# Set-up, linear attention and experts of a two-layer transformer merged into one part with four written orders

## The chip, the cores and the metric

The kernel runs on one core of a Trainium2 chip. The metric is the device time of one execution in microseconds (us), median over runs. The engines are TensorE (PE in the profile, its weight loads PEld), VectorE (DVE), ScalarE (ACT), GpSimd (POOL) and SyncE (SP), which here only issues DMAs. Each has its own queue and works it off strictly in the order in which the program wrote it; semaphores hold them together.

## The reference, cut to what matters

`x` is (4, 1024, 128), fp32. Two layers of attention and feed-forward follow each other, each with adaptive layernorm. What the change touches is layer 0:

```python
mod = (silu(L0_c) @ L0_wmod).reshape(4, 6, 1, -1)     # sa, ca, ga, sb, cb, gb; the same for layer 1
ga = (2 * (ga >= 0) - 1) * maximum(abs(ga), 0.25)      # gb too
h = layernorm(x) * (1 + ca) + sa
q = softmax(split_heads(h @ Wq + bq), axis=-1) * s     # 16 heads of 8
k = softmax(q, axis=-2) * s
ctx = einsum('bhnd,bhne->bhde', k, split_heads(h @ Wv + bv))
x = x + ga * (merge(einsum('bhnd,bhde->bhne', q, ctx)) @ Wo + bo)
h = layernorm(x) * (1 + cb) + sb
comb = ...   # sigmoid scores, best 2 of 4 groups, best 4 of 16 experts
x = x + gb * (sum over experts of comb * (silu(h @ w1.T) * (h @ w3.T)) @ w2.T, and one shared expert)
```

Layer 1 (a windowed attention and two blocks of a local transformer) stays as it is.

## The kernel before

`X` holds all 32 tiles of 128 tokens in SBUF. A batch has eight tiles. Each part is a block of its own, and all engines meet at its end.

`setup` (from L192) loads constants and `X`, multiplies the conditioning by `wmod` and spreads the rows of it that are needed over 128 partitions (`rowB`), then clamps the first gate `ga` there as a 128x512 tile on VectorE. `modT` holds the same values as columns.

`linear_attention` (from L272) loops twice over a pair of batches, `bi`; the two batches of a pair are two streams. A pair is worked in two turns `g` of four tiles for each stream. In a turn VectorE takes layernorm statistics (L140, L146) and applies them (L162), GpSimd computes the inverse root (L153, L154), TensorE transposes (L174), ScalarE scales and shifts (L399), TensorE projects q and v (L430), VectorE adds the biases (L354, L355), takes and subtracts the maximum (L358, L359), ScalarE exponentiates (L403), VectorE sums, inverts and divides (L366 to L368), ScalarE exponentiates again for k (L407) and TensorE transposes q (L436) and accumulates the context (L441). Each phase is written for both streams before the next. After the second turn the contexts are scaled (L372, L373), multiplied by `Wo`, gated, and applied to q (L457), and VectorE adds product and bias to `X` (L386, L387). GpSimd meanwhile splits the expert weights `w1`, `w3` into a high and a low part (L496, L498), clamps gate rows as 128x512 tiles (L504 to L508) and multiplies `w2` by the gate `gb` for all four batches (L512).

`moe` prepares batch 0 (statistics, L785, transposes, logits, L726) and then runs a loop of 72 units `s`: four batches of two halves of 512 tokens, nine units of 128 hidden columns each. A unit is `up(s)`, six fp32r matmuls (L665 to L667), `silu(s)` (L739), `product(s)` (L839), on GpSimd `weigh(s)` by the combine weights (L607), and two units later `down(s)` (L681). The routing of batch `r` runs on VectorE in small operations (scores L791, compares L801 and L804, counts L812 and L815, weights L832); TensorE turns its result (L653), and SyncE stores it and spreads it over the partitions as `cb` (L581). Batches 2 and 3 are routed ten units ahead by `lead(s, k)`. Batch 0 is routed at once, while TensorE has only units 0 and 1 to do, and batch 1's layernorm, transposes and logits come after unit 1.

## Time and profile before

| | |
|---|---|
| median of 3 runs | 1479.02 us (1478.18 to 1479.35) |
| the profiled execution | 1477.64 us, span 1475.9 us, mean granted clock 0.942 |
| busy, share of the span | PE 87%, PEld 68%, DVE 74%, ACT 58%, POOL 51% |

The span reaches from the first to the last instruction. The granted clock is a share of full speed: 1.0 is 2.4 GHz, 0.5 is 1.2 GHz. Of an idle engine the profile names what ended its wait. In a timeline a row joins equal instructions that follow each other; `x8` is their count, and the bracket is the idle time before the first and its releaser.

### The profile page before, as it was taken

What the parts mean: (1) busy time and instruction counts of PE and PEld (TensorE: products, weight loads), DVE (VectorE), ACT (ScalarE), POOL (GpSimd) and SP (SyncE); (2) the same over time, 40 slices, a digit from 0 to 9 for tenths busy, and PEclk for the clock granted to TensorE, in tenths of its full rate; (3) what the DMA queues carried; (4) which work ended last, traced back from release to release, by engine and by line L of the source; (5) the groups of instructions that cost most, each with busy time, mean ns of one, the idle gap of its engine ahead of it and who ended that gap; (6) DMA issues with size and microseconds to landing.
All of it is one profiled execution on the core that took longest, in us unless ns stands there. A gap on an engine that the chain in (4) does not pass through costs nothing.

```text
span 1475.9 us, 39803 instructions
## 1 busy us (share of the span) xinstructions
PE 1290.8 (87%) x16160; PEld 999.5 (68%) x16160; DVE 1090.9 (74%) x2423; ACT 850.9 (58%) x2023; POOL 753.2 (51%) x565
## 2 busy tenths in 40 slices
PE   4545899996999999998389999998888999999887
PEld 3434787884777777776268888875556888887655
DVE  4776766734787888877488998985577989988475
ACT  1222232222566666665288998984347999998521
POOL 1752455443243443433388777771255877787100
PEclk7786899996999999999599999999999999999999
DMA  4000553330000000000300000100101001000011
GB/s 141 0 0 1 116 116 85 68 81 12 3 3 3 3 4 3 3 3 3 95 8 10 14 19 10 29 6 11 34 14 30 9 10 25 8 8 2 14 36 52
DMA packets 61842, 40.39 MB, mean 27 GB/s; under 512 B 41312, under 2 KB 51808, under 8 KB 61664
## 3 DMA queue, kind: packets, MB, share of 16 engines
q1 hardware_dynamic: 61664, 37.88, 10.7%
q8 instruction: 128, 2.10, 0.6%
q14 instruction: 50, 0.41, 0.1%
HBM read 27.12 MB, written 2.36 MB: 20 GB/s over the span
## 4 chain that ended last, share of the span: by engine, by line
PE 35%; SPq 7%; DVE 4%; ACT 2%; POOL 2%; issue 1%; DMA 1%; DVEq 0%; POOLq 0%; ACTq 0%
SPq L1469 5%; PE PS L1996 4%; PE PS L1973 4%; PE PS L1982 4%; PE PS L1946 4%; PE PS L2016 4%; PE PS L1914 3%; PE PS L1916 3%; PE PS L1915 3%; PE PS L2076 2%; PE PS L2007 2%; PE PS L1961 2%; PE PS L2085 1%; POOL rn L1536 1%; ACT e_pm L1822 1%
## 5 line engine op out<-in xcount | busy, mean ns | idle before, releaser
L1543 POOL TENSOR_TENSOR rot<-qk,sinl 128x1024 f32<-128x1024 f32 x64 | 218.0, 3407 | 109.3 <-DVE qk L1643 109.3
L1536 POOL TENSOR_TENSOR rn<-ss,neghalf 128x16 f32<-128x16 f32 x64 | 210.3, 3286 | 39.1 <-DVE ss L1636 38.2
L1822 ACT ACTIVATE e_pm<-PS,e_mx 128x128 f32<-128x128 f32 x512 | 151.6, 373 | 18.7 <-DVE e_mx L1627 18.7
L1102 DVE TENSOR_REDUCE d_mx<-PS 128x4 f32<-128x576 f32 x128 | 96.9, 757 | 66.4 <-PE PS L1246 63.4
L607 POOL TENSOR_TENSOR uu<-uu,cb 128x512 f32<-128x512 f32 x64 | 82.8, 1296 | 89.8 <-DVE uu L839 87.9
L739 ACT ACTIVATE sg<-PS 128x512 f32<-128x512 f32 x72 | 43.0, 597 | 134.1 <-PE PS L667 134.1
L1165 ACT ACTIVATE pa<-PS 128x512 f32<-128x512 f32 x128 | 76.4, 597 | 61.8 <-PE PS L1255 61.7
L1914 PE MATMUL PS<-wqkv_hi,e_h_hi 128*128 128x512 f32 x192 | 91.4, 476 | 19.0 <-DVE e_h_lo L1620 19.0
L1246 PEld LDWEIGHTS PS<-kx,d_q 32*64 32x64 f32 x2048 | 66.4, 133 | 48.8 <-issue 32.9
L1627 DVE TENSOR_REDUCE e_mx<-PS 128x8 f32<-128x1024 f32 x64 | 78.2, 1222 | 28.1 <-PE PS L1973 28.1
L839 DVE TENSOR_TENSOR uu<-sg,PS 128x512 f32<-128x512 f32 x72 | 49.4, 687 | 66.8 <-ACT sg L739 66.0
L1246 PE MATMUL PS<-kx,d_q 32*64 32x256 f32 (+1 forms) x2048 | 98.0, 306 | 0.0
L1781 ACT ACTIVATE qk<-PS 128x512 f32<-128x512 f32 x128 | 76.9, 603 | 35.9 <-PE PS L1916 35.8
L1996 PEld LDWEIGHTS PS<-e_vv,e_pa 128*64 128x64 f32 x2048 | 70.0, 137 | 38.0 <-issue 32.3
L1041 POOL TENSOR_TENSOR zvareps<-zmeanvar,epsv 128x1 f32<-128x1 f32 x32 | 6.1, 191 | 175.0 <-DVE zmeanvar L1095 175.0
L2076 PE MATMUL PS<-fT,f_w 128*128 128x512 f32 x192 | 93.9, 622 | 0.0
L1996 PE MATMUL PS<-e_vv,e_pa 128*64 128x65 f32 x2048 | 87.8, 228 | 4.8 <-ACT e_pa L1829 4.8
L1106 DVE TENSOR_TENSOR pm<-PS,d_mx 128x512 f32<-128x512 f32 x128 | 88.5, 691 | 4.4
L1872 ACT ACTIVATE gate<-PS,f_b 128x512 f32<-128x512 f32 x48 | 33.0, 688 | 100.1 <-PE PS L2076 100.1
L1175 ACT ACTIVATE pm<-pm 128x512 f32<-128x512 f32 x128 | 80.6, 630 | 15.0 <-DVE pp L1107 14.5
L1255 PE MATMUL PS<-ident,pm 128*128 128x128 f32 x512 | 80.2, 280 | 7.4 <-ACT pp L1177 7.3
L1643 DVE TENSOR_TENSOR qk<-qk,rn 128x1024 f32<-128x1024 f32 x64 | 77.9, 1217 | 7.8 <-ACT qk L1781 2.9
(246 smaller groups left out, 3645.8 us busy)
## 6 DMA issues: line engine op xcount, KB each, us to landing
cb<-comb_rows SPq DMA_DIRECT2D x32, 512.0 KB, 9.1
X<-in_L_attn_x SPq DMA_DIRECT2D x4, 512.0 KB, 7.3
zs<-Z SPq DMA_DIRECT2D x64, 32.0 KB
zg<-Z SPq DMA_DIRECT2D x16, 128.0 KB
out_x<-X SPq DMA_DIRECT2D x8, 256.0 KB, 2.5
zs<-Z SPq DMA_DIRECT2D x64, 31.8 KB
zg<-Z SPq DMA_DIRECT2D x16, 127.0 KB
wqkv<-in_e_wqkv SPq DMA_DIRECT2D x2, 768.0 KB, 4.4
```

The costliest lines, as they stand in the source:

```text
L607: pool.tensor_tensor(uu[:, s % 4, :], uu[:, s % 4, :], cb[:, g % 2, ORDER[k], :], ALU.mult)\
L1102: chain(dve.tensor_reduce(mx[:, par, :, :], s, AX.X, ALU.max))
L1106: dve.tensor_tensor(out, s[:, :, :, 0:2 * W1], bc(mx[:, par, :, :], 3, 2 * W1), ALU.subtract)
L1175: last = act.activation(p, p, ACT.Exp)
L1246: last = pe.matmul(o, q[r:r + 32, b, rows], kk, start=False, stop=True, skip_group_check=True)
L1255: last = pe.transpose(PS[:, TBANK, j * P:(j + 1) * P], pm[:, g % 2, 4 * (j // 2) + 2 * e + j % 2, :], ident[:, :])
L1536: pool.tensor_tensor(rn[:, v % 2, :], ss[:, v % 2, :], c.neghalf[:, :], ALU.pow).then_inc(rn_ready.sem, 1)
L1543: pool.tensor_tensor(rot[:, :, :, :], x, bc(sinl[:, t, :, :], 2, H2), ALU.mult).then_inc(rot_ready.sem, 1)
L1822: last = act.activation(pm[:, v % 2, h, r, j, :], PS[:, SBANK + r, at * KEYS2:(at + 1) * KEYS2], ACT.Exp, bias=mx[:, v % 2, r, at:at + 1])
L1914: pe.matmul(to, h_hi[:, v % 4, :], w_hi[:, third(k)], start=True, stop=False)
L1996: last = pe.matmul(PS[rows, OBANK + h, at * (DH2 + 1):(at + 1) * (DH2 + 1)], pa[:, h, i, rows], vv[:, b, 4 * h + at, (t + 1 + blk) % 2, :] ...
L2076: last = pe.matmul(PS[:, 2 * (k % 2) + i, :], w1[:, HC * i + j, :], fT[:, g % 2, :], start=True, stop=True)
```

## The change

`setup`, `linear_attention` and `moe` become one function `front` with one block. `x` arrives in five DMAs, and the four tiles of half a batch are a chunk `n`, 0 to 7, so batch 0 is chunks 0 and 1. The chunks are no longer worked in pairs: each engine has one order written out by hand, in which the steps of up to three chunks stand between each other. Further:

- The gates are clamped as columns in `modT` (`gates`), and the rows of `rowB` are made from the clamped columns: two of them by TensorE and ScalarE, four by a transpose, a store and a spreading load.
- Layernorm is applied on ScalarE (`apply`, and `m_apply` for the experts of batches 0 and 1) with the negative mean times the inverse root from GpSimd.
- `bq` is added by a bf16 matmul of three parts into the bank of q; `bv` is added to the scaled context; `bo` before the gate. One residual addition instead of two.
- The first routing stands between the chunks' steps. Its sigmoid comes from an exponential and a reciprocal. Batch 1's layernorm starts before the loop, its routing eight units ahead (`LEAD1`) instead of at once.
- `w1` and `w3` are split in eight halves (`split(k)`). `w2` is gated for batch 0 before the loop, for the others in three pieces each inside it, at units 3 to 5 of the batch before.
- Buffers are shared: `q`, `ek`, the applied layernorm and `hl` lie in the second half of `cb`, `wmod` in `w2g`; `h_hi` and `h_lo` are rings of four halves.
- ScalarE issues the four DMAs for conditioning, identity, `bq` and `wqv`.

The orders up to the loop, read off the diff, with the arguments in brackets (chunk, batch, layer, or batch and half):

```
TensorE: mods(0), turn(0), gate_rows(), values(0), turn(1), queries(0), values(1), turn(2), queries(1), mods(1),
  values(2), context(0), turn(3), queries(2), turn_q(0), context(1), turn(4), values(3), turn_context(0), turn_q(1),
  weigh_context(0), queries(3), attend(0), turn(5), turn_rows(), values(4), attend(1), context(2), turn_q(2), turn(6),
  queries(4), turn_q(3), values(5), context(3), queries(5), turn_context(1), values(6), turn_x(0,0), queries(6),
  weigh_context(1), turn_q(4), logits(0,0), turn_x(0,1), attend(2), logits(0,1), attend(3), context(4), turn(7),
  context(5), values(7), queries(7), turn_context(2), weigh_context(2), turn_q(5), attend(4), context(6), attend(5),
  context(7), turn_q(6), turn_context(3), turn_comb(0), weigh_context(3), turn_q(7), attend(6), attend(7)
VectorE: condition(), stats(0), stats(1), mods(0), gates(0), stats(2), stats(3), stats(4), stats(5), maxima(0),
  shift(0), sums(0), invert(0), maxima(1), divide(0), shift(1), stats(6), sums(1), invert(1), divide(1), mods(1),
  maxima(2), identb, shift(2), scale_context(0), gates(1), sums(2), invert(2), gate_context(0), divide(2), maxima(3),
  residual(0), shift(3), stats(7), sums(3), m_stats(0,0), invert(3), divide(3), residual(1), maxima(4), shift(4),
  m_stats(0,1), scale_context(1), maxima(5), sums(4), shift(5), invert(4), divide(4), sums(5), maxima(6),
  gate_context(1), invert(5), shift(6), divide(5), residual(2), sums(6), scores(0), invert(6), groups(), residual(3),
  kept(), scale_context(2), contest(0), divide(6), contest(1), maxima(7), contest(2), gate_context(2), shift(7),
  contest(3), sums(7), residual(4), invert(7), divide(7), count(), residual(5), scale_context(3), weights(0),
  gate_context(3), m_stats(1,0), residual(6), residual(7), m_stats(1,1)
ScalarE: apply(0), features(0), apply(1), copy_v(0), features(1), apply(2), exp_q(0), features(2), copy_v(1),
  apply(3), exp_k(0), exp_q(1), apply(4), copy_v(2), exp_k(1), features(3), copy_rows(), copy_qT(0), exp_q(2),
  copy_context(0), apply(5), copy_v(3), features(4), copy_qT(1), exp_k(2), features(5), exp_q(3), apply(6), copy_v(4),
  copy_qT(2), copy_rowsT(), exp_k(3), m_apply(0,0), features(6), exp_q(4), copy_v(5), copy_qT(3), m_apply(0,1),
  exp_q(5), copy_context(1), whole(0,0), high(0,0), exp_k(4), whole(0,1), exp_q(6), copy_qT(4), exp_logits(),
  high(0,1), apply(7), exp_k(5), copy_v(6), features(7), exp_k(6), copy_context(2), copy_v(7), exp_q(7), copy_qT(5),
  exp_k(7), copy_qT(6), copy_context(3), take_comb(0), copy_qT(7), m_apply(1,0), m_apply(1,1)
GpSimd: rstd(0), rstd(1), bias_rows(), rstd(2), rstd(3), rstd(4), out_bias(), split(0), split(1), split(2), split(3),
  rstd(5), split(4), split(5), rstd(6), split(6), rstd(7), m_root(0,0), split(7), m_root(0,1), split_h(0,0),
  gate_down(), split_h(0,1), m_root(1,0), m_root(1,1)
```

The functions on which the times hang (`turn` transposes, `values` and `queries` project, `turn_q` transposes q, `context` accumulates, `maxima` to `divide` are the softmax):

```diff
+    def gate_down(self, pool, c, b, k):
+        part = slice(3 * k, 3 * k + 3)
+        pool.tensor_tensor(self.w2g[:, b, part, :], self.w2[:, part, :], bc(c.rowB[:, c.L0GB, b, :], 1, 3),
+                           ALU.mult).then_inc(self.w_gated.sem, 1)
...
+        spare = ex.cb[:, 1, :, :]
+        q, ek, xl = (spare[:, 2 * k:2 * k + 2, :].rearrange("p s (t d) -> p s t d", d=D) for k in range(3))
+        hl = spare[:, 6:8, :]
...
+                x = A["L0_attn_x"]
+                sp.dma_start(X[:, 0:G4, :], x[0][0:GT].rearrange("(t p) d -> p t d", p=P)).then_inc(x_loaded[0].sem, 16)
+                sp.dma_start(wmod[0], A["L0_wmod"]).then_inc(mod_loaded[0].sem, 16)
+                sp.dma_start(X[:, G4:TB, :], x[0][GT:S].rearrange("(t p) d -> p t d", p=P)).then_inc(x_loaded[1].sem, 16)
+                sp.dma_start(X[:, TB:2 * TB, :], x[1].rearrange("(t p) d -> p t d", p=P)).then_inc(x_loaded[2].sem, 16)
+                sp.dma_start(bv[:, :], A["a_bv"].partition_broadcast(P)).then_inc(c_loaded.sem, 16)
+                sp.dma_start(bmask[:, :], A["c_bmask"]).then_inc(c_loaded.sem, 16)
+                sp.dma_start(bo[:, :], A["L0_attn_bo"].partition_broadcast(P)).then_inc(c_loaded.sem, 16)
+                sp.dma_start(wo[:, :], A["L0_attn_Wo"]).then_inc(c_loaded.sem, 16)
+                sp.dma_start(X[:, 2 * TB:3 * TB, :], x[2].rearrange("(t p) d -> p t d", p=P)).then_inc(x_loaded[3].sem, 16)
+                sp.dma_start(ex.w1, A["w1T"]).then_inc(ex.up_loaded.sem, 16)
+                sp.dma_start(ex.w3, A["w3T"]).then_inc(ex.up_loaded.sem, 16)
+                sp.dma_start(X[:, 3 * TB:4 * TB, :], x[3].rearrange("(t p) d -> p t d", p=P)).then_inc(x_loaded[4].sem, 16)
+                sp.dma_start(wmod[1], A["L1_wmod"]).then_inc(mod_loaded[1].sem, 16)
+                sp.dma_start(ex.w2[:, :, :], A["w2T"]).then_inc(ex.down_loaded.sem, 16)
...
+                def rstd(n):
+                    pool.wait_ge(l_stats.sem, l_stats.at(n + 1))
+                    pool.tensor_scalar(lnm[:, n, :], lmv[:, n, :, 0], -1.0, None, ALU.mult)
+                    steps(pool.tensor_tensor(lve[:, n, :], lmv[:, n, :, 1], c.epsv[:, :], ALU.add))
+                    steps(pool.tensor_tensor(lrs[:, n, :], lve[:, n, :], c.neghalf[:, 0:G4], ALU.pow))
+                    pool.tensor_tensor(lnm[:, n, :], lnm[:, n, :], lrs[:, n, :], ALU.mult).then_inc(l_rstd.sem, 1)
...
+                    if s // (2 * NU) + 1 < B and s % (2 * NU) in (3, 4, 5):
+                        ex.gate_down(pool, c, s // (2 * NU) + 1, s % (2 * NU) - 3)
...
+                def queries(n):
+                    if n:
+                        pe.wait_ge(q_shifted.sem, q_shifted.at(n))
+                    else:
+                        pe.wait_ge(bias_ready.sem, 3)
+                    pe.matmul(PS[:, QB, :], sel[:, :], bqr[:, :, :].rearrange("p t d -> p (t d)"), start=True, stop=False,
+                              skip_group_check=True)
+                    for i in range(G4):
+                        last = pe.matmul(PS[:, QB, i * P:(i + 1) * P], hl[:, n % 2, i * P:(i + 1) * P], wqv[:, 0:D],
+                                         start=False, stop=True, skip_group_check=True)
+                    last.then_inc(q_psum.sem, 1)
...
+                def attend(n):
+                    pe.wait_ge(wctx_ready.sem, wctx_ready.at(n // 2 + 1))
+                    pe.wait_ge(qT_copied.sem, qT_copied.at(n + 1))
+                    if n % 2:
+                        pe.wait_ge(resid.sem, resid.at(n))
+                    for i in range(G4):
+                        last = pe.matmul(PS[:, YA, i * P:(i + 1) * P], qT[:, n % G4, i * P:(i + 1) * P], wctx[:, :],
+                                         start=True, stop=True)
...
+                def apply(n):
+                    act.wait_ge(l_rstd.sem, l_rstd.at(n + 1))
+                    if n >= 2:
+                        act.wait_ge(l_xT.sem, l_xT.at(n - 1))
+                    for i in range(G4):
+                        last = act.activation(xl[:, n % 2, i, :], chunk(n, i), ACT.Identity, scale=lrs[:, n, i:i + 1],
+                                              bias=lnm[:, n, i:i + 1])
...
+                def exp_logits():
+                    act.wait_ge(logit_ready.sem, logit_ready.at(1))
+                    act.activation(th[:, :, :].rearrange("p t e -> p (t e)"), PS[:, LB, 0:TB * E], ACT.Exp,
+                                   scale=-1.0).then_inc(tanh_ready.sem, 1)
...
+                def gates(l):
+                    gate, sign = c.modT[:, l, 2:6:3, :], sgn[:, l, :, :]
+                    steps(dve.tensor_scalar(sign, gate, 0.0, 2.0, ALU.is_ge, ALU.mult))
+                    steps(dve.tensor_scalar(sign, sign, 1.0, None, ALU.subtract))
+                    steps(dve.tensor_tensor(gate, gate, sign, ALU.mult))
+                    steps(dve.tensor_scalar(gate, gate, 0.25, None, ALU.max))
+                    dve.tensor_tensor(gate, gate, sign, ALU.mult).then_inc(mod_ready.sem, 1)
...
+                def scale_context(b):
+                    dve.wait_ge(ctx_done.sem, ctx_done.at(2 * b + 2))
+                    if b == 0:
+                        dve.wait_ge(c_loaded.sem, 16 * 4)
+                    steps(dve.reciprocal(rk[:, :], PS[:, CB, D:D + 1]))
+                    steps(dve.scalar_tensor_tensor(cx[:, :], PS[:, CB, 0:D], rk[:, 0:1], bv[:, :], ALU.mult, ALU.add))
+                    dve.tensor_tensor(cx[:, :], cx[:, :], bmask[:, :], ALU.mult).then_inc(ctx_scaled.sem, 1)
+
+                def gate_context(b):
+                    dve.wait_ge(wctx_psum.sem, wctx_psum.at(b + 1))
+                    if b == 0:
+                        dve.wait_ge(bias_ready.sem, 4)
+                        dve.wait_ge(rows_copied.sem, 2)
+                    steps(dve.tensor_tensor(wctx[:, :], PS[:, YA, D:2 * D], bo[:, :], ALU.add))
+                    dve.tensor_tensor(wctx[:, :], wctx[:, :], c.rowB[:, c.L0GA, b, :], ALU.mult).then_inc(wctx_ready.sem, 1)
...
                         up(s)
-                    if s == 1:
-                        turn_comb(0)
-                        turn_x(1, 0)
-                        turn_x(1, 1)
-                        logits(1)
+                    if s < 2:
+                        turn_x(1, s)
+                    if s == 2:
+                        for st in STREAMS:
+                            logits(1, st)
```

## Rows read from the trace of the kernel before

**Rows 1.** windows; length, busy PE, PEld, DVE, ACT, POOL, PEclk, DMA share, GB/s
```profile
0.00:24.00 24.00, 9.48 (x48) 6.93 (x48) 6.97 (x16) 2.40 (x14) 0.20 (x4) 0.87 0.46 123
24.00:126.00 102.00, 52.98 (x268) 45.63 (x268) 73.96 (x190) 25.15 (x42) 53.97 (x40) 0.76 0.07 22
126.00:136.30 10.30, 5.28 (x24) 4.87 (x25) 4.62 (x24) 2.89 (x4) 5.81 (x8) 0.55 0.01 3
136.30:162.00 25.70, 17.09 (x58) 14.02 (x59) 18.46 (x88) 6.80 (x11) 8.51 (x9) 0.58 0.41 84
162.00:340.50 178.50, 168.81 (x1028) 145.94 (x1026) 106.75 (x265) 47.73 (x82) 89.74 (x74) 1.00 0.38 84
```

**Rows 2.** who waited for whom, 24 to 136 us: total, times, longest
```profile
DVE q L354 <- PE PS L430: 16.0, 4, 6.0
```

**Rows 3.** groups of VectorE by line, 24 to 126 us
```profile
L368 DVE TENSOR_TENSOR q<-q,rs 128x512 f32<-128x512 f32 x8 | 9.2, 1153 | 0.3
...
L140 DVE BATCH_NORM_STATS2 stat<-X 128x6 f32 x32 | 6.5, 276 | 0.1
...
L386 DVE TENSOR_TENSOR X<-X,PS 128x512 f32 x8 | 5.5, 682 | 0.5 <-PE PS L457 0.4
...
L358 DVE TENSOR_REDUCE mx<-q 128x64 f32<-128x512 f32 x8 | 5.4, 674 | 0.0
...
L367 DVE RECIPROCAL rs<-rs 128x64 f32<-128x64 f32 x8 | 4.4, 553 | 0.3
...
L146 DVE BATCH_NORM_AGGREGATE meanvar<-stat 128x2 f32<-128x6 f32 x32 | 2.5, 152 | 0.2
...
L373 DVE SCALAR_TENSOR_TENSOR cx<-PS,rk,bmask 128x128 f32<-128x128 f32 x4 | 1.4, 350 | 0.1
```

**Rows 4.** timeline, start of the expert loop: start, length, engine, line
```profile
136.32 0.77 PE L665 MATMUL PS<-h_hi,w_hi 128*128 128x512 f32 x1
...
136.90 0.50 DVE L791 TENSOR_SCALAR score<-th 128x128 f32<-128x128 f32 x1 [4.82 <-ACT th L726]
...
146.21 0.39 DVE L832 SCALAR_TENSOR_TENSOR comb<-beaten,score 128x128 f32<-128x128 bf16 x1
...
146.65 0.47 PE L653 MATMUL PS<-ident,comb 128*128 128x128 f32 x1 [5.32 <-DVE comb L832]
...
158.62 1.27 POOL L607 TENSOR_TENSOR uu<-uu,cb 128x512 f32<-128x512 f32 x1 [1.92 <-DMA cb<-comb_rows]
...
162.02 1.05 PE L681 MATMUL PS<-w2g,uu 128*128 128x128 f32 x8
```

**Rows 5.** lines L368 and L801: duration min/median/max in ns
```profile
L368 DVE TENSOR_TENSOR q<-q,rs x8: 691/851/1826, 44.0 to 113.7; 128x512 f32<-128x512 f32 x8
...
L801 DVE TENSOR_TENSOR wins<-biased x60: 168/228/1390, 140.2 to 275.4; 128x120 bf16<-128x120 f32 x4, 128x112 bf16<-128x112 f32 x4, 128x104 bf16<-128x104 f32 x4, 128x96 bf16<-128x96 f32 x4
```

**Rows 6.** line L985, ScalarE
```profile
L985 ACT ACTIVATE hT<-PS,modT x4: 449/453/457, 346.6 to 348.2; 128x128 f32<-128x128 f32 x4
```

**Rows 7.** groups of ScalarE by line, 24 to 126 us
```profile
L407 ACT ACTIVATE ek<-q 128x512 f32<-128x512 f32 x8 | 5.0, 631 | 13.5 <-DVE q L368 13.2
```

**Rows 8.** timeline, TensorE in linear attention
```profile
45.61 1.93 PE L441 MATMUL PS<-v,ek 128*128 128x129 f32 x8
...
48.59 1.06 PE L441 MATMUL PS<-v,ek 128*128 128x129 f32 x8
```

**Rows 9.** windows inside linear attention, columns as in rows 1
```profile
55.00:63.00 8.00, 0.00 (x0) 0.00 (x0) 7.83 (x10) 1.26 (x2) 7.75 (x5) 0.74 0.00 0
63.00:70.00 7.00, 6.19 (x28) 5.54 (x28) 3.99 (x8) 2.73 (x5) 7.00 (x3) 0.57 0.00 0
```

**Rows 10.** window inside the loading of X, columns as in rows 1
```profile
8.00:10.00 2.00, 1.95 (x3) 0.92 (x4) 0.13 (x1) 0.00 (x0) 0.00 (x0) 1.00 1.18 291
```

**Rows 11.** groups of GpSimd by line, 24 to 136 us
```profile
L512 POOL TENSOR_TENSOR w2g<-w,rowB 128x1152 f32<-128x1152 f32 x4 | 11.6, 2930 | 0.1
```

More of the change, by code:

```diff
@@ new lines, in _ @@
+                copy_qT(2)
+                copy_rowsT()
+                exp_k(3)
+                m_apply(0, 0)
+                features(6)
+                exp_q(4)
+                copy_v(5)
+                copy_qT(3)
+                m_apply(0, 1)
+                exp_q(5)
+                copy_context(1)
+                whole(0, 0)
+                high(0, 0)
+                exp_k(4)
+                whole(0, 1)
+                exp_q(6)
+                copy_qT(4)
+                exp_logits()
@@ L762, in _ @@
                         high(lead(s, 9), 1)
-                    if lead(s, 10) not in (None, 1):
+                    if lead(s, 10):
                         tanh(lead(s, 10))
@@ new lines, in stats, with maxima @@
+                def stats(n):
+                    if n < 2 or n % 2 == 0:
+                        dve.wait_ge(x_loaded[n if n < 2 else n // 2 + 1].sem, 16)
+                    for i in range(G4):
+                        last = dve.bn_stats(lst[:, n, i, :], chunk(n, i))
+                    steps(last)
+                    for i in range(G4):
+                        last = dve.bn_aggr(lmv[:, n, i, :], lst[:, n, i, :])
+                    last.then_inc(l_stats.sem, 1)
+                def maxima(n):
+                    dve.wait_ge(q_psum.sem, q_psum.at(n + 1))
+                    steps(dve.tensor_reduce(mx[:, n % 2, :], PS[:, QB, :].rearrange("p (t e) -> p t e", e=DH0), AX.X, ALU.max))
@@ L806, in compare, with contest, count @@
                     steps(last)
-                def count(won, n, first, last):
+                def contest(part):
+                    compare(wins, biased, E, range(4 * part, 4 * part + 4))
+                def count(won, n):
                     k = n // 2
-                    if first:
-                        steps(dve.tensor_tensor(beaten[:, 0:k, :, 0:n], won[:, 0:k, :, :], won[:, k:2 * k, :, :], ALU.add))
-                    while last and k > 1:
+                    steps(dve.tensor_tensor(beaten[:, 0:k, :, 0:n], won[:, 0:k, :, :], won[:, k:2 * k, :, :], ALU.add))
+                    while k > 1:
                         k //= 2
@@ new lines, in _ @@
+                mods(0)
+                gates(0)
+                stats(2)
+                stats(3)
+                stats(4)
+                stats(5)
+                maxima(0)
+                shift(0)
+                sums(0)
+                invert(0)
+                maxima(1)
+                divide(0)
+                shift(1)
+                stats(6)
+                sums(1)
+                invert(1)
+                divide(1)
+                mods(1)
+                maxima(2)
+                dve.wait_ge(w_loaded.sem, 16 * 2)
@@ new lines, in _ @@
+                dve.tensor_copy(identb[:, :], ident[:, :])
+                shift(2)
+                scale_context(0)
+                gates(1)
+                sums(2)
+                invert(2)
+                gate_context(0)
+                divide(2)
+                maxima(3)
+                residual(0)
+                shift(3)
+                stats(7)
+                sums(3)
+                m_stats_of(0, 0)
+                invert(3)
+                divide(3)
+                residual(1)
@@ new lines, in _ @@
+                maxima(4)
+                shift(4)
+                m_stats_of(0, 1)
+                scale_context(1)
+                maxima(5)
+                sums(4)
+                shift(5)
+                invert(4)
+                divide(4)
+                sums(5)
+                maxima(6)
+                gate_context(1)
+                invert(5)
+                shift(6)
+                divide(5)
+                residual(2)
+                sums(6)
+                scores(0)
+                invert(6)
@@ new lines, in _ @@
+                contest(1)
+                maxima(7)
+                contest(2)
+                gate_context(2)
+                shift(7)
+                contest(3)
+                sums(7)
+                residual(4)
+                invert(7)
+                divide(7)
+                count(wins, E)
+                residual(5)
+                scale_context(3)
+                weights(0)
+                gate_context(3)
+                m_stats_of(1, 0)
+                residual(6)
+                residual(7)
```

834 lines of the change are left out of this document (464 added, 370 removed).

## Prediction

> **What bounds the kernel now.** I read the windows of the trace first, cut at the borders of the parts, then the waits inside the slackest of them, then its groups by line for the durations. Set-up takes 24.0 us, linear attention 102.0 us and the preparation of the experts 10.3 us, and only at 136.3 us does TensorE start the first expert product [rows 1]. Then follow 25.7 us in which it is busy 17.1 us, and 178.5 us in which it is busy 168.8 us at a granted clock of 1.00 [rows 1]. The reader is to see two regimes. From 162 us on TensorE sets the pace and nothing is to be had there by reordering. Before 136.3 us nothing is full: in linear attention VectorE, the fullest engine, is busy 74.0 of 102.0 us, TensorE 53.0, ScalarE 25.2. The waits say why: VectorE's largest is for TensorE's projections, 16.0 us in 4 waits [rows 2]; the code shows the reason: two streams go through one phase together and then both stand in the next. So the stretch before 136.3 us is bound by a chain of phases, with VectorE's work as the floor under it.
>
> **VectorE's work after the change.** A chunk is four tiles, as a stream's turn was before. Its eight steps per chunk become: statistics 1.2 us (four of L140 in 0.8 busy, four of L146 in 0.3 to 0.4), two reductions at 0.67, the shift at 0.69 (a pass over 128x512, as the others), the reciprocal at 0.55, the division at 0.69 undisturbed, the residual at 0.68 [rows 3]. That is 5.15 us; eight chunks give 41.2. The bias of q (now a matmul), the bias of v (folded into the context), the second residual addition and the layernorm's application (now on ScalarE) are gone from VectorE. Statistics for two batches of the experts: 4 x 1.2 = 4.8. Contexts: five operations of at most 0.35 a batch (L373) [rows 3], 1.6 with the shorter reciprocal, so 6.4. The first routing ran from 136.90 to 146.60 us on VectorE, where TensorE's transpose had waited 5.32 us for it [rows 4], 9.7 us; the score now needs a reciprocal of 128x128 in addition, two times 0.55: 10.8. Set-up: some 16 operations on vectors of 4 to 24 columns. The trace has none so small there; the smallest compares are 0.168 us [rows 5], so about 3.0, against 7.0 us busy in the old set-up [rows 1]. Sum 66.2 us, of which the last statistics and the last residual (1.9) come after `residual(6)` and don't hold the first expert product: 64.3.
>
> **What disturbs it.** The division took from 0.691 to 1.826 us, mean 1.153 [rows 3, 5]; the long ones are those beside GpSimd's splits and weight gating. GpSimd keeps most of that work, now in halves, so I add 8 x (1.153 - 0.691) = 3.7. The bounds are nothing and, if a good part of the 30 compares of the routing are met as well (0.228 alone, 1.390 at worst [rows 5]), 11 more.
>
> **ScalarE.** Old linear attention kept it busy 25.2 us [rows 1]. It gains 12 applications of four 128x128 activations: one for each of the eight chunks, four for the experts' first two batches. The nearest row, 0.453 us each [rows 6], gives 1.8 a chunk, 21.7 in all; eight copies of v no dearer than an exponential (0.631 [rows 7]), 5.0; row copies 1.3. With the experts' 2.9 that stood in the 10.3 us before [rows 1] it comes to 56 us. It stays below VectorE, but it is no longer free: an exponential can stand behind an application, up to 1.8 us.
>
> **TensorE.** An fp32 matmul of 128 columns costs 0.24 us at the low level of the clock (eight in 1.93) and 0.13 at the high one (eight in 1.06) [rows 8]. A chunk needs 24 of them, eight chunks 192: 46 us at the low level. Eight bias matmuls of 512 columns (four times the columns in bf16, some 0.5), the contexts, gate rows, two transposed halves and 16 logit products come on top, another 19: some 65 us at the low level, 35 at the high one. The clock goes by what came before: 55 to 63 us TensorE does nothing, and from 63 to 70 it is granted 0.57, mostly 1.2 GHz of its 2.4; over the linear attention 0.76 [rows 1, 9]. At the low level TensorE would thus be nearly as full as VectorE.
>
> **Walking the queues.** Now I go down the four orders written out in the diff with these durations, TensorE at the low level. The start: DMA moved 291 GB/s while X and the weights came in [rows 10], so 256 KB of X and the conditioning are there at about 4.6 us (an estimate: 2 us to issue and start, 0.9 for the bytes, the rest for the table load and the first small steps) and all 4.8 MB that SyncE issues first in about 18 us. That is before `mods(1)` and `stats(6)` are reached near 20 us, so the 13 DMAs in one queue cost nothing; at half that rate they would cost 10. VectorE then waits: before `maxima(0)` 2.2 us (the first projection's chain), four waits under 1 us up to chunk 2, 1.8 around `gate_context(0)` and `residual(0)`, 2.3 before `maxima(4)`, 1.4 around `scale_context(1)`, 2.3 before `residual(2)` (TensorE has a half's logits and a transpose ahead of `attend(2)`), 0.9 before the scores, 1.0 before the last context, the rest small: 16 us. Part of the front will run at 2.4 GHz, for TensorE is busier than it was; I take back 4, leaving 12. First expert product: 4.6 + 64.3 + 3.7 + 12 + 1.1 (`attend(7)`) = 85.7, say 86 us, against 136.3. **Gain 50.3.**
>
> The Trainium skill (TensorE: Matmul & The Clock Gate, HAM oscillation) says that a matmul engine which keeps waiting between bursts is throttled to half clock again and again. The trace agrees for the wait of 8 us above. If the rule held for the whole new front, whose order leaves TensorE many short waits, the 4 us would not be taken back and the sum below would be 1425.5; it is rival 1 in a mild form.
>
> **The start of the expert loop.** Before, from the first product at 136.32 to `down(1)` at 162.02 is 25.7 us. In it TensorE waits 5.3 us for the routing, transposes and routes batch 1 only then, and multiplies at the low level nearly throughout [rows 4, 1]. After, the routing is done some 5 us before `up(0)`, for `gate_context(3)`, `attend(6)`, `residual(6)` and `attend(7)` follow it. The combine rows were ready for GpSimd 12.0 us after the routing's end (146.60 to 158.62 [rows 4]), hence about 7 us after `up(0)`, when `weigh(1)` is just due: that DMA is hidden. What is left: `silu(0)` stands behind `m_apply(1, 1)`, which waits for the last residual and its statistics, to about 5.7 us after `up(0)` (0.7 and 1.2 on VectorE, 1.6 on GpSimd, 1.8 on ScalarE, and the hand-overs), plus a table load; then four products (1.3 to 2.6 each), two transposes, 16 logit products and one `down`: 12 us at the high level, 18 to 20 at the low. I take 16.5. **Gain 9.2.** In the loop, `gate_down` puts nine pieces on GpSimd, each a third of 2.93 [rows 11]: 9 us. GpSimd is busy 89.7 of 178.5 [rows 1], so most hides; three in a row reach 2.3 us a unit, about a unit's time, and hold back VectorE's small operations for batch 1, whose routing also starts two units later. **Loss 2**, bounds 0 and 9.
>
> **Sum.** 50.3 + 9.2 - 2 = 57.5 us. The profiled execution took 1477.64 (span 1475.9), 1.4 below the median of 1479.02. So span 1418.4, its own time 1420.1, and the median **1421.5 us**. The part after the experts (from 340.5 on, 1135 us) is untouched; the gates of layer 1 arrive by DMA long before.
>
> **Rivals.**
> 1. *TensorE at 1.2 GHz throughout, its fixed order binding.* For: TensorE's 65 us at that level, and the single bank for q, which lets `queries(n+1)` in only after `shift(n)`. Against: 1.00 was granted as soon as it had worked without pause (162 us on). The 4 come back, 3 more waits, loop start 18: 57.5 - 7 - 1.5 = 49 gained, 1430.
> 2. *GpSimd blocks VectorE.* For: the ranges of [rows 5]. Against: most of the split is over before the compares. The 11 us above: 1432.
> 3. *Everything overlaps better than I walked it.* TensorE warm early, waits 5 instead of 12, no blocking, loop start 12, no loss in the loop: 57.5 + 7 + 3.7 + 4.5 + 2 = 75, 1404.
> 4. *The other side: chunks don't overlap.* If each chunk's chain had to end before the next can use its banks and halves, one chunk costs applied, turned, scaled, projected (6.2), softmax with two exponentials (5.2), context and attend with residual (4.2), so 15.6, and eight cost 125; with 6 before and 5 behind it the first product comes at 136 and, with rival 1's loop start and the 9 on GpSimd, the time is 1479 or up to 1483. It decides only when a chunk costs over 15.3 us. Against: `turn(n+1)` to `queries(n+1)` stand ahead of chunk n's softmax in every queue, and the halves are two deep.
>
> **Chances.** My forecast 0.45 (own range 1412 to 1431), rival 1 0.2, rival 2 0.1, rival 3 0.2, rival 4 0.03, something unnamed 0.02. The 8-in-10 range takes in rivals 1 to 3 with the bounds of `gate_down` and the waits: 1403 to 1441. A measurement of this kernel can tell some 0.2% (3 us) from no change; all but rival 4 and half of the unnamed are faster by far more: faster 0.96, same 0.02, slower 0.02.
>
> **What would show it.** Right: `up(0)` at 80 to 92 us; VectorE over 75% busy before it; no wait of GpSimd on the combine DMA over 2 us; 14 to 19 us from `up(0)` to `down(1)`; 178 to 182 us from there to the last addition; the rest as long as before. Wrong: a gap of TensorE on a DMA near 20 us, ScalarE over 60 us before `up(0)`, clock 0.5 across the front, or a `weigh` in the first batch that is late for `down`.

## The result and the profile after

| | before | changed |
|---|---|---|
| median of 4 runs each | 1478.92 us (1478.18 to 1479.35) | 1424.81 us (1422.77 to 1425.69) |
| profiled execution, span | 1475.9 us | 1423.9 us |

The ratio is 0.9633 with a 95% interval of 0.9616 to 0.9649: 54.1 us less by the medians, 52.0 by the two profiled spans. Forecast were 1421.5 us and 57.5 us.

In some executions of the changed kernel and of the experiments TensorE stays at the low level of its clock for up to 90 us at the start of the windowed attention; the ratios leave out the slow ones among them, and the profiles of `e3_silu_first`, `e4_routing_after`, `b1_three_moves` and `b2_filled` are such ones, so no difference in time is read from these behind the last addition of the experts, save for the products that `b2_filled` adds there.

The windows of the changed kernel, cut at 24 us, at the first expert product, at `down(1)` and at the last addition, columns as in [rows 1]:

```profile
0.00:24.00 24.00, 14.14 (x84) 13.50 (x85) 12.32 (x66) 10.79 (x22) 16.77 (x39) 1.00 0.70 217
24.00:80.80 56.80, 45.81 (x323) 41.18 (x323) 52.39 (x162) 34.87 (x74) 22.65 (x35) 0.91 0.07 23
80.80:97.40 16.60, 11.19 (x59) 9.21 (x58) 3.92 (x12) 9.33 (x17) 6.80 (x9) 0.90 0.70 168
97.40:283.00 185.60, 170.97 (x1028) 146.12 (x1026) 115.35 (x274) 47.64 (x82) 99.25 (x84) 1.00 0.36 77
...
0.00:80.84 80.84, 60.00 (x406) 54.72 (x407) 64.71 (x227) 45.66 (x95) 39.46 (x73) 0.94 0.25 81
```

The 52.0 us of the spans come from four places [rows 1 for before]: the first product comes 55.5 us earlier (136.3 to 80.8), from there to `down(1)` 9.1 us are saved (25.7 to 16.6), the loop from there takes 7.2 us more (178.4 to 185.6), and the part behind the experts 5.4 us more (1135.4 to 1140.8). The second line is the one to look at: VectorE is busy 52.4 of 56.8 us, where it was 74.0 of 102 before. It has become the bound of the front, and TensorE's clock there is 0.91 instead of 0.76.

Who waited for whom, start to first product:

```profile
POOL l_negmean L398 <- DVE l_meanvar L991: 22.5, 2, 21.9
...
PE PS L470 <- DMA wqv<-in_a_wqv: 8.6, 1, 8.6
...
DVE ce L910 <- ACT ce L821: 3.2, 1, 3.2
...
DVE l_stat L933 <- DMA X<-in_L_attn_x: 2.5, 1, 2.5
...
DVE mx L941 <- PE PS L512: 2.3, 1, 2.3
```

VectorE's large waits all lie before 20 us: for the table load and exponential of the conditioning, for the second chunk of `X`, for the first projection. After 24 us none is longer than 1.0 us. GpSimd stands 21.9 us with nothing to do before the statistics of batch 1.

VectorE's groups by line, 14 to 81 us: the division (it answers to L368 in [rows 3]), the reciprocal, the context's mask, its gate, and the score:

```profile
L961 DVE TENSOR_TENSOR cb<-cb,rs 128x512 f32<-128x512 f32 x8 | 6.7, 834 | 0.2
...
L957 DVE RECIPROCAL rs<-rs 128x64 f32<-128x64 f32 x8 | 4.4, 545 | 0.1
...
L969 DVE TENSOR_TENSOR cx<-cx,bmask 128x128 f32<-128x128 f32 x4 | 2.2, 544 | 0.1
L977 DVE TENSOR_TENSOR wctx<-wctx,rowB 128x128 f32<-128x128 f32 x4 | 2.1, 516 | 0.1
...
L1015 DVE TENSOR_SCALAR score<-th 128x128 f32<-128x128 f32 x1 | 1.0, 1011 | 0.0
```

The timeline of the changed kernel: first the start of the loop (all engines), then VectorE and GpSimd in units 3 and 4, where batch 1 is routed:

```profile
84.69 0.20 POOL L401 TENSOR_TENSOR l_negmean<-l_negmean,l_rstd 128x4 f32<-128x4 f32 x1
...
84.93 1.65 ACT L776 ACTIVATE xn<-X,l_negmean,l_rstd 128x128 f32<-128x128 f32 x4 [2.28 <-POOL l_negmean L401]
86.59 1.28 ACT L814 ACT_TABLE_LOAD   x1
87.89 0.60 ACT L814 ACTIVATE m_work<-PS 128x512 f32<-128x512 f32 x1
...
88.52 0.69 DVE L1066 TENSOR_TENSOR m_work<-m_work,PS 128x512 f32<-128x512 f32 x1 [5.50 <-ACT m_work L814]
...
89.97 1.09 PE L562 MATMUL PS<-ident,xn 128*128 128x128 f32 x4 [5.20 <-ACT h_hi L790]
...
98.86 0.22 DVE L1013 TENSOR_SCALAR score<-th 128x128 f32<-128x128 f32 x1
99.11 1.34 DVE L1018 TENSOR_TENSOR biased<-score,gbias 128x128 f32<-128x128 f32 x1
100.48 0.29 DVE L1019 TENSOR_REDUCE gmax<-biased 128x32 f32<-128x128 f32 x1
...
101.67 1.26 DVE L1026 TENSOR_TENSOR gwins<-gmax 128x8 bf16<-128x8 f32 x1
102.85 1.09 DVE L1029 TENSOR_TENSOR gwins<-gmax 128x16 bf16<-128x16 f32 x2
...
100.26 1.05 POOL L218 TENSOR_TENSOR w2g<-w,rowB 128x384 f32<-128x384 f32 x1
101.57 1.33 POOL L422 TENSOR_TENSOR m_work<-m_work,cb 128x512 f32<-128x512 f32 x1 [0.26 <-DVE m_work L1066]
102.86 1.04 POOL L218 TENSOR_TENSOR w2g<-w,rowB 128x384 f32<-128x384 f32 x1
```

Read the two stalls. At the start, ScalarE waits 2.28 us for GpSimd's root for `m_apply(1, 1)`, then loads a table, and only then runs `silu(0)` at 87.89, 7 us after `up(0)`; TensorE stands 5.20 us and drops to the low level for the next products. In the loop, VectorE's compare of 8 columns at 101.67 takes 1.26 us and ends (102.93) where GpSimd's weighing ends (102.90); elsewhere the same compare takes 0.17.

Most of what is longer behind the experts, where the code is the same, lies in the closing feed-forward: two rows of 24 `down` passes there take 4.57 and 4.35 us instead of 2.94, each after TensorE had waited over 2.6 us; in the kernel before only one does (4.58). Timeline of the changed kernel:

```profile
1363.69 2.94 PE L2385 MATMUL PS<-f_w,f_uu 128*128 128x128 f32 x24 [2.05 <-DVE f_uu L2004]
...
1375.96 4.57 PE L2385 MATMUL PS<-f_w,f_uu 128*128 128x128 f32 x24 [3.66 <-DVE f_uu L2004]
...
1397.60 4.35 PE L2385 MATMUL PS<-f_w,f_uu 128*128 128x128 f32 x24 [2.63 <-DVE f_uu L2004]
```

### The profile page after: what moved, and what is told of

Its sections match the earlier page's. It is cut to its first block, busy times and chain, and to the rows that moved or that the text cites. A ratio compares the mean times of both kernels' runs of the same rounds, so it can differ in the third digit from the quotient of the medians.

```text
span 1423.9 us, 39853 instructions
## 1 busy us (share of the span) xinstructions
PE 1278.2 (90%) x16225; PEld 992.1 (70%) x16225; DVE 1064.5 (75%) x2355; ACT 869.0 (61%) x2064; POOL 740.8 (52%) x595
## 4 chain that ended last, share of the span: by engine, by line
PE 35%; SPq 7%; DVE 5%; POOL 2%; ACT 2%; issue 2%; DMA 1%; DVEq 0%; POOLq 0%; ACTq 0%
SPq L1769 5%; PE PS L2296 4%; PE PS L2282 4%; PE PS L2273 4%; PE PS L2246 4%; PE PS L2316 4%; PE PS L2214 3%; PE PS L2216 3%; PE PS L2215 3%; PE PS L2307 2%; PE PS L2261 2%; PE PS L2385 1%; PE PS L2376 1%; POOL rn L1836 1%; DVE qk L1943 1%
## 5 line engine op out<-in xcount | busy, mean ns | idle before, releaser
L422 POOL TENSOR_TENSOR m_work<-m_work,cb 128x512 f32<-128x512 f32 x64 | 83.1, 1300 | 87.3 <-DVE m_work L1066 87.3
L814 ACT ACTIVATE m_work<-PS 128x512 f32<-128x512 f32 x72 | 43.0, 597 | 136.8 <-PE PS L604 136.8
L1066 DVE TENSOR_TENSOR m_work<-m_work,PS 128x512 f32<-128x512 f32 x72 | 49.6, 688 | 77.2 <-ACT m_work L814 76.4
L1555 PE MATMUL PS<-ident,pm 128*128 128x128 f32 x512 | 80.2, 280 | 7.5 <-ACT pp L1477 7.4
```

The costliest lines, as they stand in the source:

```text
L422: pool.tensor_tensor(uu[:, s % 4, :], uu[:, s % 4, :], cb[:, g % 2, ORDER[k], :], ALU.mult)\
```

## The experiments

All are made from the changed kernel. Theory: the front is bound by VectorE, once the chunks overlap; what the loop lost is GpSimd's gating of `w2`, which holds up VectorE's short instructions; what the first units lost is ScalarE's order. Times in the profile are read against the changed kernel: `up(0)` 80.8, `down(1)` 97.4, last addition 283.1.

**c0_changed_again.** The changed kernel, unaltered.

> The changed kernel itself, unaltered, beside the other runs of this group. Theory (in the windowed attention TensorE is given its full clock back at a moment that differs between executions, for any kernel that comes there like this one): up(0) at 79 to 83, last addition at 281 to 286 us in the profile, and a spread of the single times of over 5 us. Rival (the spread of 1419.9 to 1454.6 us in the first three experiments came with their edits): all times between 1422 and 1428.

Ratio 0.9629 (0.9610 to 0.9649). `up(0)` at 80.66, `down(1)` at 97.39, last addition at 283.04, all within 0.2 us of the first profile. Over all profiles whose front is unedited (this one, the first, e2 and e3) `up(0)` lies between 80.2 and 82.2, and wherever the loop is unedited (six profiles, e6 left out) `down(1)` to the last addition takes 185.6 to 185.7 us. The stretch of the loop resolves far smaller effects than whole times do, which were 1424.57, 1425.46, 1425.84 and 1447.36 us here: an outlier comes without any edit, as the theory said. The stretch before the loop is less steady, as `b1_three_moves` shows below.

**e5_chunk_by_chunk.** On TensorE, ScalarE and VectorE the order by hand becomes a loop:

```diff
-turn(0); gate_rows(); values(0); turn(1); queries(0); values(1); turn(2); queries(1); ...
+for n in range(NC): turn(n); values(n); queries(n); turn_q(n); context(n)   # and the pair's steps when n is odd
```

> Same part without barriers, same instructions, but TensorE, ScalarE and VectorE take the chunks one after the other, each to its end, with the first routing as one block behind chunk 4. Theory (the overlap of chunks is the gain, not the missing barriers): one chunk's chain of some 11 us, eight times, with the additions of four batches and the routing: up(0) at 112 to 128 us, VectorE near 55% busy before it, total 1457 to 1473. Rival (the barriers and the separate set-up were the cost, and queues overlap by themselves): up(0) at 84 to 95 us, total 1429 to 1440.

The ratio is 1.0263 (1.0243 to 1.0283): slower than the kernel before. Its window up to `up(0)`:

```profile
0.00:178.71 178.71, 99.08 (x406) 84.89 (x407) 62.49 (x219) 48.67 (x95) 35.84 (x69) 0.59 0.20 55
```

VectorE has much the same work (62.5 us busy) and needs 178.7 us for it, so it is busy 35% and not near 55%; TensorE's same passes take 99 us instead of 60 at a clock of 0.59. The rival is out, and the theory was too mild by 50 us: it had left out that TensorE becomes slower when it is idle so much, which is at most 39 us of the 98 by which `up(0)` comes later; the rest isn't separated. In the merged block the order is worth 98 us. What the block would be worth with the old order, two streams phase by phase, no run shows.

**e6_norm_on_vector.** The applications of the first layernorm go back to VectorE.

```diff
-act.activation(xl[:, n % 2, i, :], chunk(n, i), ACT.Identity, scale=lrs[...], bias=lnm[...])
+dve.tensor_scalar(xl[:, n % 2, i, :], chunk(n, i), lmv[...], lrs[...], ALU.subtract, ALU.mult)
```

> The 32 applications of the first layernorm go back from ScalarE to VectorE (a subtract and multiply of 128x128, about 0.28 us each, 9.0 us in all). Theory (VectorE bounds the front): up(0) 7 to 10 us later, at 88 to 91, with VectorE over 88% busy before it. Rival (VectorE's 16 us without work before up(0) take them in): up(0) at 80 to 84.

Ratio 0.9707 (0.9684 to 0.9730), `up(0)` at 93.25, 12.4 us later. The group, up to 93 us:

```profile
L936 DVE TENSOR_SCALAR cb<-X,l_meanvar,l_rstd 128x128 f32<-128x128 f32 x32 | 12.7, 458 | 0.8 <-POOL l_negmean L370 0.8
```

VectorE's busy time before `up(0)` grows by 9.5 us, from 64.7 to 74.2, and all of it arrives there; 2.9 us of waits come on top (16.1 to 19.1, TensorE's clock 0.87 instead of 0.94). So VectorE bounds the front, and the rival is out, though VectorE is busy 80% as before and not over 88%. The 12.7 us of the group are more than the 9.5, since the long instructions beside GpSimd are now among the applications (median 0.341 us, up to 1.423), and the context's mask, its gate and the score are shorter for it (1.2, 1.7 and 0.2 us instead of 2.2, 2.1 and 1.0).

**e4_routing_after.** The first routing goes behind `residual(7)`, `turn_comb(0)` behind `attend(7)`, `take_comb(0)` behind `copy_qT(7)`.

```diff
-scores(0); invert(6); groups(); residual(3); kept(); ...; count(wins, E); residual(5); scale_context(3); weights(0)
+...; residual(6); residual(7); scores(0); groups(); kept(); contest(0..3); count(wins, E); weights(0)
```

> VectorE's first routing (13.3 us of work from scores to weights) is taken from between chunks 5 to 7 and put behind residual(7). Theory (VectorE has no gaps there, it is 95% busy from 20 to 76 us, so the routing only changes its place): up(0) comes 11 to 14 us earlier, at 67 to 70; the routing still ends near 81 us, but the table of weights then needs some 12 us to the first weigh as in the kernel before, so down(1) is 2 to 5 us later than 97.4 and the total 1427 to 1430. Rival (the routing filled gaps between the chunks): up(0) comes less than 5 us earlier, down(1) 10 us or more later, total 1434 to 1438.

Neither. `attend(7)` starts at 73.78 instead of 79.96, so of the routing's work 6.2 us stood on the path and the rest filled waits; alone, from 75.55 to 86.20, it takes 10.65 us. `up(0)`, which now stands behind `turn_comb(0)`, an effect the expectation forgot, comes at 86.6, and TensorE, idle meanwhile, works the first units at a clock of 0.59:

```profile
70.00:86.60 16.60, 3.58 (x24) 2.81 (x24) 13.44 (x66) 0.87 (x2) 1.64 (x4) 0.74 0.00 0
86.60:105.00 18.40, 16.39 (x58) 13.80 (x58) 2.89 (x10) 9.48 (x18) 6.67 (x8) 0.59 0.57 133
```

`down(1)` and the last addition come 7.6 us later; ratio 0.9644 (0.9624 to 0.9664).

**e7_rows_later.** `gate_rows()` moves from before `values(0)` to behind `queries(1)`.

> gate_rows (16 passes, 3.8 us) goes from ahead of values(0) to behind queries(1) on TensorE; VectorE waits 2.3 us for queries(0) at 17.7 to 20.0. Theory (that wait is TensorE's order): first maxima at 17.5 to 18.5 instead of 20.0, and up(0) 1 to 2.3 us earlier. Rival (what the first chunk gains is lost again, since turn_context(0) and gate_context(0) then wait for the rows): up(0) within 0.7 us of the changed kernel's in this group.

VectorE's timeline:

```profile
17.65 0.69 DVE L941 TENSOR_REDUCE mx<-PS 128x64 f32<-128x512 f32 x1
```

The first maxima start at 17.65 us (18.0 and 18.1 in b2 and b1, which have this edit too) where six profiles without it have 19.4 to 20.3 (e5 and e6, which change what stands ahead of it, left out); `up(0)` comes at 78.41 (77.9 and 79.5), and the last addition at 280.98, 2.1 us earlier. The ratio, 0.9667 (0.9618 to 0.9715), is too wide to show it, the anchors do.

**e1_gates_front.** The nine pieces of `gate_down` leave the loop and fill GpSimd's 21.9 us.

```diff
 split_h(0, 1)
+for b in range(1, B):
+    for k in range(3): ex.gate_down(pool, c, b, k)
 m_root(1, 0)
```

> The nine scalings of the experts' down weights (gate_down, batches 1 to 3, 1.05 us each) leave the loop and run on GpSimd right after split_h(0, 1), in the 21.9 us in which it waits for residual(6). Theory (these pieces, beside VectorE's routing and ahead of the next weigh, are what the loop lost): from down(1) to the last addition 185.6 us becomes 178 to 181, up(0) comes 0 to 4 us later because VectorE's routing is now beside them, total 1420 to 1424. Rival (the loss comes from the order of the routing of batch 1 and the units around it, not from the pieces): the stretch stays at 184 to 186 and the total is 1425 to 1429.

From `down(1)` to the last addition 179.4 us instead of 185.6: the theory's 6.2 us. But `up(0)` comes 6 us later, at 86.8, and `down(1)` 20.2 us after it instead of 16.6, at a clock of 0.68 instead of 0.90. So the last addition is 3.4 us later, and the ratio is 0.9643 (0.9609 to 0.9676), no gain; the forecast total, 1420 to 1424, was missed. The timeline beside the moved pieces:

```profile
59.12 6.75 POOL L218 TENSOR_TENSOR w2g<-w,rowB 128x384 f32<-128x384 f32 x7
...
62.03 1.03 DVE L1031 TENSOR_TENSOR gwins<-gmax 128x8 bf16<-128x8 f32 x1
62.97 1.03 DVE L1028 TENSOR_TENSOR gwins<-gmax 128x8 bf16<-128x8 f32 x1
```

Each compare of 8 columns takes 1.03 us, about one piece (1.04), where the changed kernel needs 0.17 at the same place: one instruction of VectorE gets through for one of GpSimd's. The six compares of this group take 5.7 us (60.25 to 65.91), where e4 needs 0.6 for them (77.44 to 78.06). The pieces cost what short instructions meet them, wherever they lie.

**e2_gates_late.** So they go where VectorE has few short instructions.

```diff
-if s // (2 * NU) + 1 < B and s % (2 * NU) in (3, 4, 5):
+if s // (2 * NU) + 1 < B and s % (2 * NU) in (11, 13, 15):
```

> The three pieces of gate_down of each of batches 1 to 3 go from units 3, 4 and 5 of the batch before, where VectorE runs the short instructions of the routing, to units 11, 13 and 15, where it has only sums and applications of the layernorm. Theory (a piece costs what VectorE's short instructions wait behind it, about 1 us for each one that meets it): from down(1) to the last addition 180 to 183 us instead of 185.6. Rival (a piece costs because it delays GpSimd's next weighing): 185 to 188 us.

Ratio 0.9589 (0.9565 to 0.9614). `down(1)` to the last addition:

```profile
96.90:276.28 179.38, 170.07 (x1028) 146.00 (x1026) 110.50 (x275) 47.61 (x82) 98.80 (x84) 1.00 0.36 79
```

It takes 179.4 us, 6.3 less and even less than forecast, with the same work on GpSimd; VectorE's busy time falls from 115.4 to 110.5. The pieces are also further apart now, so the length alone doesn't decide between theory and rival. TensorE's waits in this stretch do (L602 in the changed kernel, then in e2, L622 in both):

```profile
PE PS L602 <- DVE m_work L1066: 10.8, 18, 1.1
PE PS L622 <- POOL m_work L422: 2.6, 3, 1.0
...
PE PS L602 <- DVE m_work L1066: 5.4, 14, 1.1
PE PS L622 <- POOL m_work L422: 2.5, 3, 1.0
```

What falls is the wait for VectorE's `product`, from 10.8 to 5.4 us (the kernel before had 5.7); the wait for GpSimd's weighing stays. The rival (a delayed weighing) is out.

**e3_silu_first.** `m_apply(1, 1)` goes behind `silu(0)`, `whole(1, 0)` and `high(1, 0)`.

> silu(0) goes ahead of m_apply(1, 1) on ScalarE, which now waits there 2.28 us for GpSimd's root and then loads a table. Theory (ScalarE's order holds the first units): silu(0) at about 84.5 instead of 87.9, from up(0) to down(1) 12.5 to 14.5 us instead of 16.6, total 1421 to 1422.5. Rival (turn_x(1, 1) on TensorE, behind whole and high of stream 0, waits as long as before): from up(0) to down(1) 16 to 17 us, total 1424 to 1426.

`silu(0)` starts at 85.17, 2.94 after `up(0)` instead of 7.05; from `up(0)` to `down(1)` it is 12.6 us instead of 16.6, so the rival is out. Ratio 0.9606 (0.9585 to 0.9627), which by itself can't be told from the changed kernel's 0.9629.

**b1_three_moves.** e2, e3 and e7 together.

> The three moves together: gate_down at units 11, 13 and 15, silu(0) ahead of m_apply(1, 1), gate_rows behind queries(1). Theory (the three lie in different stretches and add up: 6.3, 4.0 and 2.2 us): last addition at 269 to 272 us instead of 283.0, total 1411 to 1414. Rival (they share a wait, since the first units also decide when batch 1 is routed): last addition at 273 to 277, total 1415 to 1419.

Last addition at 271.28, 11.8 us earlier than the changed kernel's, 0.7 short of the sum of the three: they add up in this profile. In that of `b2_filled`, the same kernel up to there, it is at 274.48, 8.6 us earlier: TensorE's clock falls at 85.8 us, is 0.74 instead of 0.88 from `up(0)` to `down(1)`, and that stretch takes 16.6 us instead of 12.5. Ratio 0.9559 (0.9547 to 0.9571) where the changed kernel has 0.9629: the fastest version here, 65 us under the kernel before.

**b2_filled.** b1 and 18 idle products on TensorE at the start of the windowed attention.

```diff
+for k in range(10):    # and 8 more behind the products of hrep
+    pe.matmul(PS[:, 7, :], ident[:, :], rowB[:, k % 2, :, :], start=True, stop=True)
 pe.wait_ge(w_loaded.sem, 80)
```

> The same with 18 products of 128x512 added on TensorE whose result nobody reads, 10 where it waits 5.5 us and 8 where it waits 3.9 us at the start of the windowed attention; their output is left out of the computation. Theory (TensorE's granted clock falls because it has no work there, and the moment at which it is given back differs between executions): the clock between the last addition and 60 us behind it 0.85 or more instead of 0.74, the stretch to the first maxima d_mx 1 to 3 us shorter, total 4 to 12 us less than without them, with a narrower spread. Rival (the later short waits at 299 to 306 us or the small passes bring the clock down anyway): clock 0.5 to 0.75 as before, total the same or up to 3 us more.

Ratio 0.9642 (0.9619 to 0.9664): 0.9% slower than b1. Windows of b2_filled behind the last addition (274.48):

```profile
270.00:290.00 20.00, 17.30 (x69) 10.05 (x68) 8.49 (x42) 2.10 (x5) 4.87 (x7) 1.00 0.09 22
290.00:310.00 20.00, 15.64 (x86) 8.93 (x85) 5.76 (x18) 6.12 (x16) 4.95 (x10) 0.69 0.00 1
310.00:330.00 20.00, 20.00 (x284) 13.80 (x282) 8.84 (x20) 7.69 (x20) 1.76 (x3) 0.50 0.01 2
```

In this execution the filled stretch keeps 1.00, but the clock falls in the unfilled waits after 295 us, as the rival said. The added products cost time themselves:

```profile
275.50 8.82 PE L1293 MATMUL PS<-rowB,ident 128*128 128x512 f32 x20 [1.05 <-PEq L314]
...
287.57 7.03 PE L1309 MATMUL PS<-rowB,ident 128*128 128x512 f32 x16
```

They take 8.8 and 7.0 us where the waits were 5.5 and 3.9, and the first maxima `d_mx` come 30.1 us after the last addition, where the eleven other profiles have 23.1 to 23.2. So the theory's 1 to 3 us less became 7.0 more, over half of the 12 us by which b2 is slower than b1 (0.9642 against 0.9559); the rest isn't separated. Theory and rival both missed the total. Whether a filler that fits into the waits would help is not shown.

## Why the prediction was right, step by step

- **VectorE's work before `up(0)`, 64.3 + 3.7.** The window shows 64.7 with the disturbance in it. The size of the disturbance was right by luck, for its place was not: the divisions took 8 x (0.834 - 0.69) = 1.2 us of it instead of 3.7, the context's mask and gate 1.9 (0.544 and 0.516 instead of 0.29, eight of them), the score's first step 0.8. So the work itself was 60.8 instead of 64.3; which terms were too high isn't separated. Of the 4.9 us by which `up(0)` came earlier than the sum of 85.7, 3.3 are here and 1.6 in the waits. That VectorE is the floor is shown by e6.
- **Start 4.6, waits 12, `attend(7)` 1.1.** Sum 17.7 forecast, 16.1 measured (80.8 - 64.7), but elsewhere. VectorE stood still 11.7 us before 24 us, and only 4.4 from 24 to 80.8; the walk had put all but some 7 of its waits into the second part. At the start it had no wait for the second chunk of `X` (2.5 us) and none for the conditioning's products (1.6), which TensorE could begin only at 8.6 us. Later it had the level of TensorE's clock wrong: it walked at the low one and took back 4, while 0.94 was granted up to `up(0)`. That this is the cause of the missing waits is argued, not shown by a run. With `up(0)` at 80.8 instead of 86, the gain is 55.5 instead of 50.3.
- **TensorE's work, 65 us at the low level and 35 at the high.** Both are too small, because rows were taken for matmuls. The loop over four tiles gives four fp32 matmuls, and the trace has two rows for each: eight rows in 1.93 us [rows 8] are 0.48 us a matmul at the low level, eight in 1.06 are 0.26 at the high, not 0.24 and 0.13. Only the transposes have one row. In the changed kernel the 32 matmuls of `context` show it:

```profile
L530 PE MATMUL PS<-v,cb 128*128 128x129 f32 x64 | 10.3, 312 | 1.3 <-ACT cb L748 1.3
```

  TensorE was busy 60.0 us before `up(0)` at 0.94, and the same passes took 99 us in e5 at 0.59, more than the 86 us forecast for `up(0)`. So had the clock stayed near the low level, TensorE (99 us) and not VectorE (64.7) would have been the fuller engine. The prediction had too few passes at too low a clock, and that the two offset each other is luck. ScalarE's 56 us were 45.7.
- **The clock.** The sentence on the Trainium skill (TensorE: Matmul & The Clock Gate, HAM oscillation) named 1425.5 for the case that the whole front is throttled. The trace doesn't show that case here: short waits within a front busy 60.0 of 80.8 us left 0.94. e5, busy 99 of 178.7 us in bursts, was granted 0.59 and e4 0.74 in its gap, so here the low level came with the long waits.
- **From `up(0)` to `down(1)`, 16.5 us.** 16.6, and by the mechanism named: `silu(0)` behind `m_apply(1, 1)` and a table load. e3 shows it: 4.0 us of it are this order, as long as the clock holds (12.6 and 12.5 us in the profiles of e3 and b1, 16.6 in that of b2). The combine rows' DMA was hidden, as walked; GpSimd's first weighing at 91.17 waited for no DMA.
- **`gate_down` in the loop, loss 2, bounds 0 and 9.** The mechanism was right and the size too small: 7.2 us. The step weighed GpSimd's time per unit (2.3 us, about a unit's) and named VectorE's part without a term of its own. e1 and e2 show that 6.2 to 6.3 us are the pieces, through VectorE's short instructions, each prolonged to about one GpSimd instruction. The last us is not separated; `LEAD1` and batch 1's routing two units later are candidates that weren't tried.
- **The rest, 0.** +5.4 us in the profile, and some 4.9 of it is the closing feed-forward: its second row of `down` passes at the low level costs 1.4, and TensorE waits 3.5 us more for VectorE ahead of these rows (11.1 instead of 7.6). In the profiles of c0, e1, e2, e5, e6 and e7, which have the same code there, the rest takes 1137.7 us (e6 and e7) to 1155.0 (e1). So it goes with the moments at which the clock changes; what sets these moments stays open.
- **The rivals.** 1 would have shown a clock near 0.5 across the front: it was 0.94. Its 65 us of TensorE were too few, so had the clock been low the time would have been above its 1430. 2 came true in kind, on other instructions, but at 3.9 us in all, not 11. 3 had TensorE's clock right, but its waits of 5 us were 10.4 (16.1 less the start and `attend(7)`), and it was wrong on the blocking and the loop; `up(0)` came halfway between the forecast's 86 and its 75. 4 is what e5 builds: a chunk costs some 20 us then (178.7 less start and routing, by eight), and the time is above the kernel before.
- **The signs.** Those for the front, the combine DMA and the first units held. Two failed: from `down(1)` to the last addition 185.6 us instead of 178 to 182, and the part behind the experts 5.4 us longer instead of as long.

The deviations of the gain, +5.2, -0.1, -5.2 and -5.4, make 57.5 into the 52.0 of the spans; that the median was met within 3.3 us is in part luck, for the first and the third cancel.

## What to carry to other kernels

Merging parts doesn't pay by itself: in one block without barriers, but chunk by chunk, the kernel ran slower than the one before with its barriers and its two streams, and it became faster only when the steps of several chunks stood between each other. Then the fullest engine's sum is the floor, here VectorE's 64.7 of 80.8 us. Before pricing an engine from rows, count how many rows one instruction of the source leaves in the trace. Before an order is fixed, put GpSimd's TENSOR_TENSOR work beside long or PSUM-fed instructions of VectorE, not beside a row of short ones, and look at each first unit of a pipeline for work of the next batch that stands ahead of it. When whole times scatter by more than the effect, compare anchors in the trace (first product, last addition): here the stretch of the loop repeated within 0.1 us. A stretch in which the clock can fall doesn't repeat so well (12.5 and 16.6 us for the same order in b1 and b2).

## What the runs showed of the hardware

- VectorE's TENSOR_TENSOR and TENSOR_SCALAR whose operands all lie in SBUF can be prolonged beside GpSimd's TENSOR_TENSOR: a compare of 8 columns from 0.17 to 1.03 and 1.26 us, an application of 128x128 from 0.312 to 1.423 (e6). Those with a PSUM operand aren't: the shift took 0.679 to 0.693 us over its eight, the residual 0.675 to 0.689, `product` 0.673 to 0.725 over its 72; nor the reciprocal and the sums, 0.545 and 0.676 in the mean. The Trainium skill (SBUF — State Buffer, Who interferes with whom) states such a rule: an instruction of VectorE with two SBUF inputs contends with a GpSimd instruction that reads SBUF, and one with at most one SBUF input, outside certain fast modes, doesn't. By that rule the trace agrees for the compares, the shift and the sums; whether the applications and the score, which have one such input and were prolonged, ran in a fast mode, no run shows. With it, the step on `gate_down` could have counted the 30 compares beside the three pieces and not only GpSimd's time.
- TensorE can be kept at the low level while it is busy without a break. In the windowed attention the changed kernel got the full clock back within the second of such windows (0.61 there, 1.00 in the third), e1 only in the fourth, after 40 us at 0.50 with PE busy 19.8 and 20.0 of 20 us. Windows of `e1_gates_front` from the last addition on:

```profile
286.45:306.45 20.00, 7.97 (x25) 5.54 (x26) 9.71 (x49) 3.29 (x10) 5.36 (x12) 0.55 0.09 22
306.45:326.45 20.00, 19.82 (x225) 13.29 (x229) 9.06 (x21) 9.08 (x23) 3.54 (x7) 0.50 0.01 2
326.45:346.45 20.00, 20.00 (x285) 14.41 (x277) 9.03 (x21) 7.46 (x20) 2.23 (x4) 0.50 0.01 2
346.45:366.45 20.00, 19.76 (x359) 14.57 (x352) 12.52 (x32) 10.02 (x29) 4.19 (x8) 0.74 0.01 2
```

The kernel before, in the runs beside these experiments, stayed between 1477.89 and 1482.81 us; why it regains the clock so evenly there and the changed kernel doesn't is open, and the filler of b2, which overran the first waits, didn't mend it.
